# Residual sums, statistics and loads of finished tile groups brought into the drain of a stack and into the attention between two stacks

## The reference

```
x = x + 0.5 * stack(layernorm(x))        # "block 0"
x = x + attention(layernorm(x))          # global attention, 4 heads of 32
x = x + 0.5 * stack(layernorm(x))        # "block 1", same weights as block 0

stack(t): 6 times
    t = t + local_attention(shift_tokens(t)) @ Wo      # 16 heads of 64, window 32
    t = t + (a * gelu(gate)) @ W2                      # of shift_tokens(t), normalised
```

## Time and profile before

| what | us |
|---|---|
| median of 3 runs (lowest to highest) | 3437.93 (3436.97 to 3445.19) |
| the profiled execution's own time | 3436.08 |
| its span in the trace | 3434.3 |
| end of block 0's last sum into `stream` | 1593.1 |
| first query product of the attention (line 1182) | 1614.6 |
| last update of the attention starts | 1853.2 |
| first projection of block 1 | 1869.6 |

### The profile page before, as it was taken

How to read it: one execution, slowest core, us unless ns; L and a number is a source line. 1 busy time by engine, 2 the same in 40 slices (tenths; PEclk the granted TensorE clock), 3 DMA queues, 4 the chain that set the end, 5 groups by cost and what they waited for, 6 DMA issues and landing times. The chain is left out here.

```text
span 3434.3 us, 102986 instructions
## 1 busy us (share of the span) xinstructions
PE 3243.5 (94%) x42016; PEld 2206.8 (64%) x42016; DVE 2964.2 (86%) x5370; ACT 2531.7 (74%) x4368; POOL 2536.8 (74%) x1357
## 2 busy tenths in 40 slices
PE   6999999999999999996997899999999999999997
PEld 3666666666666666664554566666666666666664
DVE  6989999899999899983577899899999999899994
ACT  4778777877778777872575687778777878787873
POOL 6878888888888888860002888888888888788881
PEclk8999999999999999997798999999999999999998
DMA  2110010010010000002000000000000000000000
GB/s 80 49 31 2 21 31 2 20 31 2 21 31 2 21 18 2 2 2 78 1 2 1 2 2 2 33 2 2 33 2 2 33 2 2 33 2 2 2 2 13
DMA packets 31050, 53.30 MB, mean 16 GB/s; under 512 B 11510, under 2 KB 24054, under 8 KB 27254
## 3 DMA queue, kind: packets, MB, share of 16 engines
q1 hardware_dynamic: 30582, 46.71, 4.1%
HBM read 37.26 MB, written 9.44 MB: 14 GB/s over the span
## 5 line engine op out<-in xcount | busy, mean ns | idle before, releaser
L428 POOL TENSOR_TENSOR arena<-arena 128x1024 f32<-128x1024 f32 x384 | 723.2, 1905 | 400.2 <-DVE arena L531 400.2
L421 POOL TENSOR_TENSOR arena<-arena 128x1024 f32<-128x1024 f32 x384 | 907.3, 2363 | 30.1
L412 POOL TENSOR_TENSOR arena<-arena 128x1024 f32<-128x1024 f32 x384 | 767.4, 1998 | 55.9 <-ACT arena L759 42.5
L998 PE MATMUL ps_a<-w_qk,stream 128*128 128x512 f32 x1536 | 759.2, 617 | 16.4 <-DVE arena L541 11.4
L1013 PE MATMUL ps_h<-arena,w_vo 128*128 128x256 f32 x3072 | 730.7, 381 | 5.8 <-issue 4.0
L759 ACT ACTIVATE arena<-ps_a 128x512 f32<-128x512 f32 x768 | 418.8, 601 | 317.2 <-PE ps_a L998 308.1
L1013 PEld LDWEIGHTS ps_h<-arena,w_vo 128*128 128x128 f32 x3072 | 563.4, 191 | 79.0 <-issue 7.7
L541 DVE TENSOR_TENSOR arena<-ps_a,arena 128x1024 f32<-128x1024 f32 x384 | 467.1, 1216 | 54.7 <-ACT arena L759 54.6
L547 DVE TENSOR_REDUCE arena<-arena 128x16 f32<-128x1024 f32 x384 | 462.9, 1205 | 37.0 <-ACT arena L765 37.0
L991 PE MATMUL ps_t<-ident,arena 128*128 128x128 f32 x3072 | 402.7, 274 | 27.5 <-ACT arena L770 20.5
L765 ACT ACTIVATE arena<-arena 128x1024 f32<-128x1024 f32 x384 | 413.5, 1077 | 8.7 <-ACT arena L759 0.4
(11 more groups left out here) (146 smaller groups left out, 5007.0 us busy)
## 6 DMA issues: line engine op xcount, KB each, us to landing
w_qk<-fWqkv SPq DMA_DIRECT2D x12, 1024.0 KB, 5.3
vo_scr<-w_vo SPq DMA_DIRECT2D x6, 1024.0 KB, 5.6
w_vo<-vo_scr SPq DMA_DIRECT2D x6, 1024.0 KB, 7.3
arena<-fWqkv SPq DMA_DIRECT2D x6, 512.0 KB, 8.0
arena<-fWo SPq DMA_DIRECT2D x6, 512.0 KB, 8.5
w<-fW SPq DMA_DIRECT2D x12, 192.0 KB, 6.2
w<-fW SPq DMA_DIRECT2D x6, 341.0 KB, 3.3
w_scr<-w SPq DMA_DIRECT2D x6, 341.0 KB, 7.3
```

Source lines behind the costliest of these rows:

```text
L412: pool.tensor_tensor(swapped.rearrange("p (c d) -> p c d", d=DH), raw[n].rearrange("p (c d) -> p c d", d=DH), tab.unsqueeze(1).to_broadcas ...
L421: pool.tensor_tensor(r, r, swapped, ALU.add).then_inc(add_s, 1)
L428: pool.tensor_tensor(r, r, rn[u % 2][:, n * HEADS:(n + 1) * HEADS].unsqueeze(2) .to_broadcast([P, HEADS, DH]), ALU.mult).then_inc(rot_s, 1)
L998: last = pe.matmul(A[:, n * 512:(n + 1) * 512], stream[:, c0:c0 + P], w_qk[:, u // TILES % 2, off:off + 512], start=True, stop=True)
```

## The change

The work between stages is cut into finished groups. `LN_PARTS` names parts (which layer norm, first tile, end tile): part 0 is the start, parts 1 and 2 the tiles 0 to 11 and 12 to 15 before the attention, parts 3 to 6 the four groups before block 1. Statistics, root and normalisation now take a part each.

- `post` runs for groups 0 and 1 at PE's step 99, for group 2 at step 101, their adds at DVE's steps 101 and 102; in block 0 the statistics of part 1 follow at step 102, ahead of the last sum into `stream`. Only group 3 is left behind the stack.
- In odd drain steps PE's heads 8 to 11 of `mixed` come ahead of the transposes of `xn`.
- In the attention, DVE takes statistics after the updates of tiles 3, 7, 11 and 15, and normalises groups 0, 1 and 2 after the updates of tiles 5, 9 and 13.
- SP's loads for the attention and for layer 0 wait for the last unit's `red_k` and `add_k` (step 95), those of layer 1 for block 0's last `y2_ps`.
- Turned tiles before the attention go to four banks; ACT copies groups 0 to 2, then their query inputs, then group 3.

```diff
+LN_PARTS = ((0, 0, 16), (1, 0, 12), (1, 12, 16), (2, 0, 4), (2, 4, 8), (2, 8, 12), (2, 12, 16))
...
-            sp.wait_ge(post_add, 4)
+            sp.wait_ge(red_k, UNITS)
+            sp.wait_ge(add_k, UNITS)
...
-            for layer in range(2):
-                load_qk(layer)
-                load_folded(layer)
+            load_qk(0)
+            load_folded(0)
+            sp.wait_ge(y2_ps, DUOS)
+            load_qk(1)
+            load_folded(1)
...
-            pool.wait_ge(post_add, 4)
             pool.wait_ge(halo, UNITS)
-            layer_norm_rstd(1)
-            layer_norm_rstd(2)
+            for part in range(1, 7):
+                layer_norm_rstd(part)
             pool.wait_ge(g_upd, TILES)
             zero_blocks()
...
+                if st.s == UNITS + 5:
+                    post(st.block, 0)
+                    post(st.block, 1)
...
+                if st.s == UNITS + 6:
+                    post(st.block, 2)
+                    if st.block == 0:
+                        dve.wait_ge(post_add, 3)
+                        layer_norm_stats(1)
...
             steps(0, body)
-            post(0)
-
+            post(0, 3)
+            dve.wait_ge(post_add, 4)
+            layer_norm_stats(2)
+            dve.wait_ge(sw_k, UNITS)
+            dve.wait_ge(sq_k, UNITS)
             layer_norm(1)
+            layer_norm(2)
...
                 last.then_inc(g_upd, 1)
+                if t % 4 == 1 and t > 4:
+                    layer_norm(2 + t // 4)
+                if t % 4 == 3:
+                    dve.wait_ge(g_upd, t + 1)
+                    layer_norm_stats(3 + t // 4)
...
-            dve.wait_ge(g_upd, TILES)
+            layer_norm(6)
...
+                if not even and st.s > UNITS and st.duo_on(5):
+                    d = st.duo(5)
+                    pe.wait_ge(root_done, st.roots(2 * d + 4))
+                    mixed(d, range(8, 12))
...
+                if st.s == UNITS + 5:
+                    post(st.block, 2)
                 if not even and st.duo_on(7):
                     hidden(st.duo(7), 1)
+                if st.s == UNITS + 3:
+                    post(st.block, 0)
+                    post(st.block, 1)
...
             steps(0, body)
-            post(0)
-
-            pe.wait_ge(post_add, 4)
-            ln_transposes(1)
+            post(0, 3)
+            for g in range(3):
+                if g < 2:
+                    pe.wait_ge(post_add, 2)
+                else:
+                    pe.wait_ge(post_add, 3)
+                ln_transposes(1, g)
             pe.wait_ge(g_win, 16 * G_DMAS)
             for g in range(4):
+                if g == 3:
+                    ln_transposes(1, 3)
                 pe.wait_ge(ln_lo, g + 1)
```

More of the change, by code:

```diff
@@ L388, in _, with layer_norm_rstd @@
             pool.memset(half_pow[:], -0.5).then_inc(misc_done, 1)
[L390 to L395, removed]
+            def layer_norm_rstd(part):
+                n, t0, t1 = LN_PARTS[part]
+                pool.wait_ge(ln_mv, part + 1)
+                pool.tensor_scalar(rstd[:, t0:t1], mv[:, t0:t1, 1], EPS, None, ALU.add).then_inc(ln_rstd, 1)
+                pool.wait_ge(ln_rstd, 2 * part + 1)
+                pool.tensor_tensor(rstd[:, t0:t1], rstd[:, t0:t1], half_pow[:, t0:t1], ALU.pow).then_inc(ln_rstd, 1)
             def make_table(st, u):
@@ L482, in layer_norm, with post @@
                         done.then_inc(ln_norm, 1)
[L484 to L491, removed]
-                    last.then_inc(post_add, 1)
-                dve.wait_ge(post_add, 4 * n + 4)
+            def post(n, g):
+                dve.wait_ge(post_ps, 4 * n + g + 1)
+                for h, bank in enumerate(post_banks(g)):
+                    dst = x_res[:, 4 * g:4 * g + 4, h * HALF:(h + 1) * HALF]
+                    last = dve.scalar_tensor_tensor(dst, bank[:, 0:4 * HALF].rearrange("p (t d) -> p t d", t=4),
+                                                    0.5, dst, ALU.mult, ALU.add)
+                last.then_inc(post_add, 1)
             root_steps = [0]
@@ L615, in start @@
             def start(n, blk):
-                layer_norm(n)
                 for g in range(4):
@@ L868, in _, with turned, query_input @@
             steps(0, body)
-            for g in range(4):
+            def turned(g):
                 act.wait_ge(ln_ps, 4 + g + 1)
-                act.activation(g_xt[:, g * 512:(g + 1) * 512], T[g % 2][:], ACT.Copy).then_inc(ln_lo, 1)
-            act.wait_ge(halo, UNITS)
-            for g in range(4):
+                act.activation(g_xt[:, g * 512:(g + 1) * 512], ln_bank(1, g), ACT.Copy).then_inc(ln_lo, 1)
+            def query_input(g):
                 act.wait_ge(g_qin, g + 1)
@@ L879, in _ @@
                    .then_inc(g_qin_sb, 1)
+            act.wait_ge(halo, UNITS)
+            for g in range(3):
+                turned(g)
+            for g in range(3):
+                query_input(g)
+            turned(3)
+            query_input(3)
             act.wait_ge(g_win, 16 * G_DMAS)
@@ L1065, in body @@
                     mixed(d, range(0, 4))
-                if not even and st.duo_on(5):
+                if not even and st.s < UNITS and st.duo_on(5):
                     d = st.duo(5)
@@ L1263, in _ @@
             pe.wait_ge(g_smx, 2 * g_chunks[-1][-1][0] + 2)
-            ln_transposes(2)
+            for g in range(4):
+                ln_transposes(2, g)
             pe.wait_ge(zero_done, 2)
             steps(1, body)
-            post(1)
+            post(1, 3)
 def constants():
```

81 lines of the change are left out of this document (46 added, 35 removed).

## The result

| | median, us | runs | profiled execution |
|---|---|---|---|
| before, beside the changed kernel | 3437.45 | 4 (3436.22 to 3445.19) | 3436.08 |
| changed | 3406.89 | 4 (3401.12 to 3411.17) | 3401.12 |
| changed, measured again later | 3411.71 | 4 (3404.38 to 3413.67) | 3410.61 |
| before, beside that | 3441.57 | 13 (3432.19 to 3454.41) | |

The ratio is 0.9900 (0.9881 to 0.9919), and 0.9901 (0.9873 to 0.9929) the second time. The change wins some 30 us; 3422.0 with a range down to 3411 was forecast. The sign was right, the size was wrong: the sum of the prediction holds half of the gain.

The account below looks back on a forecast made before the run. Bound by waits in the passages into the attention and block 1, and the attention's first units. 5.7 - 0.5 + 8.5 + 2.2 = 15.9 us off 3436.1 gives 3420.2, 3422 as median; 8-in-10 range 3411 to 3431.

Parts of the forecast that it names:

- Step 102 and the last sum: Block 0, step 102: group 2's adds, statistics and merging of 12 tiles ahead make the last sum 1.0 us late.
- First passage: Block 0's last sum to first query product: about 14.8 us instead of 21.5; 5.7 won, bounds 3.7 and 7.5.
- the price of the three query inputs: First passage: three query inputs at 1.7 us each, 5.1 in all, the clock being low after the idle stretch.
- VectorE stopped by the power instruction: First passage: if GpSimd's power instruction for tiles 12 to 15 stops VectorE's normalisation, up to 2.94 of the 5.7 us go.
- Power on 4 values: Second passage: GpSimd's power instruction on 4 values a partition taken as 1.0 us; by count 0.73, at most 2.94.
- Attention: Statistics and normalisations inserted on VectorE between updates: only the last costs time, 0.5 us; bounds 0 and 6.6.
- Second passage: Last update to block 1's first projection: 7.1 us against 15.6, so 8.5 won; bounds 6.5 and 10.7.
- End: After block 1's last sum: 3.8 us of transposes and adds cut to 0.79 + 0.76, 2.2 us won.
- Loads, "where nothing waits for them": SyncE's loads move 70 us forward into the drain, where nothing waits for them; no gain or loss entered.
- What I took as unchanged: The two stacks, with drain effects taken as 0, the value projections' waits and block 1's ordinary start: no gain entered.
- The rival I had for the clock: Attention's first units: shifted timing spares the clock's fall, two units won back, 12.6 us, time 3409; chance 6%.
- The rival on the slower side: Attention: clock returns two value products later, four more units pay 6.3 us each, 25 us, time 3447; chance 4%.

Follow-up runs that it names:

- experiment 4: Kernel before, with only the residual sums of groups 0 to 2 (transposes and adds) moved into each stack's drain: 3432.51 us, ratio 0.9983.
- Experiment 6: Changed kernel, with SyncE's loads for the attention and layer 0 waiting for block 0's last residual sum again: 3421.9 us, ratio 0.9949.
- experiment 8: Changed kernel with extra unread TensorE products: in value stage and unit 0 (3414.19 us), also in units 1 and 2 (3403.53 us), or in each drain (3414.0 us).
- experiment 7: Changed kernel, with GpSimd's clearing put ahead of its last root: 3415.45 us, ratio 0.9921.
- experiment 3: Changed kernel, with layer norm ahead of block 1 done for all 16 tiles after the last update: 3423.83 us, ratio 0.9938.
- experiment 2: Moved `mixed` products of heads 8 to 11: first alone in the kernel before (3438.36 us), then put back in the changed kernel (3413.33 us).

## Why the prediction was wrong

By its own steps:

- **Step 102 and the last sum** (1.0 us late): the product that feeds it ends at 1588.86 and the first sum starts at 1589.85, with statistics in between. Right.
- **First passage** (14.8 from the last sum to the first query product; 12.1 measured). Three groups turned 6.9 us after the sum as forecast (to 1597.74 of 1590.80). The step that failed is the price of the three query inputs: 1.7 each, in all 5.1. They took 3.05, and 3.05 to 4.31 in the nine traces with the same order and no wait for loads. I argued that "after the idle stretch the clock is low"; but the row that I priced them from, 4.71 for four, stood behind an idle stretch of 9.99 us itself and had that clock in it: three of its four took 3.85 (experiment 4), with which the sum would have had 6.9 us here instead of 5.7. What is left of the difference is where the level rises. In the thirteen traces without the wait for loads it rose 3.2 to 6.1 us after TensorE had begun to turn tiles (3.2 and 3.9 in the changed kernel, 5.9 before), and the idle time ahead doesn't decide it: behind 9.99 us four query inputs took 4.71 and 3.99, and behind 3.27 us three took 4.31 in one trace:

```profile
1599.40 4.31 PE L1230 MATMUL ps_a<-arena 128*128 128x512 f32 x6
```

So part of the low price in the changed kernel is luck of the execution. Experiment 6 shows 5.49, where TensorE waits 2.5 us more. The remaining 0.6 is the tail (2.1 against 2.8).
- **VectorE stopped by the power instruction** (a bound): it was not. 16 normalisations took 4.16 us beside the power instruction of 1.04 at 1594.07, the same as alone (4.19). Beside the clearing four took 3.63, as forecast. The Trainium skill, page "SBUF — State Buffer", section "Who interferes with whom", gives mutual exclusion for two-port modes; the clearing agrees with it, the power instruction did not stop anything here.
- **Power on 4 values** (1.0): 1.04; on 12, 2.30. Right.
- **Attention** (0.5 lost in the last unit, nothing for the other insertions): 0.6 in the last six units of both traces, the units before unchanged. Right in the sum. In its parts not quite: the statistics of tiles 8 to 11 put 1.1 us into their unit, of which the next two give back 1.0, and the last normalisation puts in 0.9, of which the end gives back 0.5.
- **Second passage** (8.5): 8.1. Right. **End** (2.2): 2.8; the remaining store starts sooner too.
- **Loads, "where nothing waits for them"** before or after: right of the changed kernel, wrong as a statement of what the move is worth. Undone, it costs 4 to 5 us in the passage. My net sum was not hurt, since I had priced the passage without the loads.
- **What I took as unchanged** is where most of the rest of the gain was, and the second step that failed. The prediction left the drains, the value stage and the ramp of block 1 as they were, at nothing. Measured: 1.9 us from the first query product to the first row maximum, where the higher level lasted into the first scores, 1.13 us for four of them and then 1.75 at 1621.56, some 19 us behind the first query product, where before it ended in the values' last products at 1627.70 (2.56 us for 16, which take 1.95 to 2.02 at the higher level), some 14 us behind that product; 2.6 in the ramp of block 1; 0.4 to 3.4 in each drain of the two traces, 1.6 by the means of experiment 8. Only the drains have an experiment for their cause. The 1.9 are not shown to be an effect of the change: with the changed kernel's code there, the stretch took 23.3 to 23.5 us in four traces and 24.6 in two (experiments 7 and 8), and with the old code 25.3 and 25.4 in two and 24.6 in one (experiment 4). In the ramp experiment 3 takes 1.6 of the 2.6 back, and experiment 4 shows that ramp behind the long passage at 38.9 us, so chance can move it further than the change did.

Added up for the two traces of the changed kernel: 8.2 + 1.9 - 0.6 + 8.1 + 2.6 + 2.8 = 23.0, and the drains by their group means (54.1 and 52.5 us, experiment 8) 2 x 1.6 = 3.2: 26 us. 15.9 were forecast; of the 10 missing, 2.5 are the query inputs and what follows them, and 7.7 (1.9 + 2.6 + 3.2) lie in stretches that I took as unchanged. In the other seven traces with this order and no wait for loads the first passage took 14.3 to 15.3 us, so the 8.2 can be 7.1 in another execution. The rival I had for the clock was of another kind (the fall in the first units spared, 12.6 us): it did not happen, the units took 15.5, 15.7 and 14.7 as before. The rival on the slower side had a grain of truth: units at the lower level beyond the first do come, 4 to 6 us of them (experiment 7), but by chance, and with other kernels than this one as well.

Open: 26 of 30 us are placed. From the second row maximum of block 1 to its last the four traces with the long second passage (before, the first of experiment 2, and experiments 3 and 4) took 1454.7 to 1457.8 us, the ten others 1450.0 to 1454.5. In experiment 3, 2.5 us of it lie in the first unit of the stretch; in the others nothing that I found in the trace binds the difference to the change. So up to 3 or 4 us of the gain may stand there, or none.

## What to carry to other kernels

A shortened wait can give back more than its own length, because the clock level of the matmuls inside it and behind it moves too: 15.9 us were forecast from the waits, and up to 10 more were found, most of them in such stretches. But the same order of instructions gave 3.05 to 4.31 us for three products and 38.9 to 47.7 us for one ramp, so that part is a range, to be taken from several traces. Before adding a price for a low clock, look whether the row that the price comes from has the low clock in it already. And when a chain is shortened, look at every transfer that landed inside the old one: those loads become the next wait unless they move too.

## What the runs showed of the hardware

- Under the scores of 32 rows and the transposes TensorE was busy with one idle time of 0.66 us and granted 1.2 GHz from 1631.7 on in the changed kernel, until the first products with the values at 1660.28; the same scores with full-array products between them ran at 2.4 GHz (experiment 8). The row of the windows in the changed kernel:

```profile
1631.70:1640.00 8.30, 8.30 (x28) 4.15 (x24) 2.62 (x8) 2.39 (x4) 0.00 (x0) 0.50 0.00 0
```

- With TensorE work added that no one needs, 198 instead of 156 instructions, the drain of block 1 took 46.2 us in both traces that have it, and 50.6 to 53.6 in the ten without.
- One order of instructions with the same waits ran a stretch of 47.7 us in 38.9 in another execution, by the clock level alone. With the 4 to 6 us that the attention loses in some executions (experiment 7), the profiles of two kernels must be compared stretch by stretch, and their times by several runs.
- GpSimd's power instruction took 1.04, 2.30 and 2.94 us for 4, 12 and 16 values a partition, not in proportion to the count.
